# A graph layer with two interleaved parts: the bias of layer h moves from TensorE matmuls to ScalarE, and the split of h into two halves moves to VectorE

## The reference, cut to what matters

```python
h = jnp.maximum(_layernorm(x, axis=-1), 0.0)
S = feat[src]
def edge_nn(x, W, b):
    h = jax.nn.relu(x @ W.T + b)
    return jax.nn.relu(h @ W.T + b)
for r in range(W_rel.shape[0]):
    msgs = jnp.where((rel == r)[:, None], edge_nn(S, W_rel[r], b_rel[r]), msgs)
agg = jax.ops.segment_sum(msgs, dst, num_segments=n_nodes)
gates = agg @ W_ih.T + b_ih + b_hh
i, f, g, o = jnp.split(gates, 4, axis=-1)
c = jax.nn.sigmoid(i) * jnp.tanh(g)
hn = jax.nn.sigmoid(o) * jnp.tanh(c)
x = jax.nn.relu(hn @ W1.T + b1)
x = jax.nn.relu(x @ W2.T + b2)
return x @ W3.T + b3          # added to the input row
```

## Time and profile before

| | |
|---|---|
| median of three runs | 2246.85 us |
| profiled execution, its own time | 2245.49 us |
| its span | 2243.8 us |
| TensorE matmul busy | 2076.3 us, 93% |
| VectorE busy | 1759.5 us, 78% |
| ScalarE busy | 1641.5 us, 73% |
| GpSimd busy | 1182.5 us, 53% |

### The profile page before, as it was taken

One profiled execution on the slowest core, in us unless ns is written; L12 is line 12 of the kernel. 1 busy time (PEld: TensorE's weight loads), 2 busy tenths in 40 slices (PEclk: granted clock), 3 DMA queues, 4 the chain that ended last, 5 costly groups with the idle time before them and its releaser, 6 DMA issues.

```text
span 2243.8 us, 51876 instructions
## 1 busy us (share of the span) xinstructions
PE 2076.3 (93%) x14224; PEld 1397.8 (62%) x14225; DVE 1759.5 (78%) x4311; ACT 1641.5 (73%) x3373; POOL 1182.5 (53%) x917
## 2 busy tenths in 40 slices
PE   5868777768999999999999999999999999999996
PEld 4746555556666666666666666666666666445553
DVE  8657555556888888888888888888888887888886
ACT  3847555557888888888888888888888887666663
POOL 0057777777766666665666666666666644100000
PEclk7669999889999999999999999999999999999998
DMA  9975555558798988898998888898999988998886
GB/s 385 423 244 101 96 99 96 98 95 152 148 181 178 179 166 179 170 180 177 182 182 171 179 173 176 171 176 176 180 179 175 187 153 158 199 189 188 194 192 147
DMA packets 399455, 396.90 MB, mean 177 GB/s; under 512 B 262586, under 2 KB 342006, under 8 KB 393208
## 3 DMA queue, kind: packets, MB, share of 16 engines
q0 software_dynamic: 91200, 157.34, 41.7%
q1 hardware_dynamic: 305636, 238.11, 41.2%
q10 hardware_dynamic: 2516, 0.14, 0.1%
HBM read 185.88 MB, written 156.97 MB: 153 GB/s over the span
## 4 chain that ended last, share of the span: by engine, by line
PE 77%; issue 7%; DMA 6%; POOL 4%; DVE 3%; ACT 3%; POOLq 0%; DVEq 0%; ACTq 0%; SPq 0%
PE bank L1509 33%; PE bank L1456 9%; PE bank L1475 9%; PE bank L1548 6%; PE bank L1523 6%; PE bank L1492 4%; DMA agg<-summed,scatter_idx 4%; PE bank L1438 3%; PE bank L1532 3%; POOL agg L673 2%; POOL xg L657 2%; PE bank L1449 1%; PE bank L1467 1%; DMA a_lo<-row_lo 1%; PE bank L1347 1%
## 5 line engine op out<-in xcount | busy, mean ns | idle before, releaser
L673 POOL DMA_INDIRECT agg<-summed,scatter_idx x400 | 656.4, 1641 | 505.7 <-ACT summed L745 285.2
L1509 PE MATMUL bank<-a_hi,ihT 128*128 128x512 f16 x2400 | 713.8, 379 | 1.7 <-DMA a_lo<-row_lo 1.2
L657 POOL DMA_INDIRECT xg<-in_x,src_ring x384 | 414.2, 1079 | 120.8 <-issue 119.9
L1509 PE MATMUL bank<-a_lo,ihT 128*128 128x512 f16 x1200 | 454.8, 379 | 0.0
L1509 PEld LDWEIGHTS bank<-a_hi,ihT 128*128 128x128 f16 x2400 | 234.4, 98 | 211.9 <-issue 1.4
L1475 PE MATMUL bank<-relT,h_hi 128*128 x1600 | 326.2, 278 | 0.0
L1456 PE MATMUL bank<-s_hi,relT 128*128 128x256 f16 x1600 | 299.8, 282 | 0.0
L681 POOL DMA_DIRECT2D y<-in_x x100 | 133.2, 1332 | 297.7 <-DVE y L1231 287.3
L1456 PE MATMUL bank<-s_lo,relT 128*128 128x256 f16 x800 | 226.2, 283 | 0.0
L1099 DVE SCALAR_TENSOR_TENSOR s_lo<-bank,s_hi 128x512 f16<-128x512 f32 x200 | 136.6, 683 | 111.9 <-ACT s_hi L751 111.9
L1106 DVE SCALAR_TENSOR_TENSOR h_lo<-bank,h_hi 128x512 f16<-128x512 f32 x200 | 137.5, 687 | 110.5 <-ACT h_hi L772 110.5
(11 more groups left out here) (200 smaller groups left out, 4619.6 us busy)
## 6 DMA issues: line engine op xcount, KB each, us to landing
agg_in<-agg SPq DMA_DIRECT2D x100, 512.0 KB, 7.8
y<-in_x POOLq DMA_DIRECT2D x100, 512.0 KB, 9.2
out<-y SPq DMA_DIRECT2D x100, 512.0 KB
agg<-zeros SPq DMA_DIRECT2D x24, 2112.0 KB, 16.0
dst_ring<-dst_rows SPq DMA_DIRECT2D x200, 128.0 KB
agg<-summed,scatter_idx POOLq DMA_INDIRECT x400
xg<-in_x,src_ring POOLq DMA_INDIRECT x384, 5.1
src_ring<-src_slot SPq DMA_DIRECT2D x192, 1.0 KB
```

Of the source, the lines that this page charges most:

```text
L657: nc.gpsimd.indirect_dma_start(out=xg[:, k.slot(8), t, :], out_offset=None, in_=x[:, :], in_offset=bass.IndirectOffsetOnAxis(ap=rows[:, t: ...
L673: nc.gpsimd.indirect_dma_start(out=agg[:, :], out_offset=bass.IndirectOffsetOnAxis(ap=scatter_idx[:, k.slot(8), t:t + 1], axis=0), in_=sum ...
L1509: last = nc.tensor.matmul(N_C[c % 2][:, 0:UNIT], lhs, rhs, start=i == 0, stop=i == len(todo) - 1)
```

## The change

In the joint part the two bias matmuls of layer h go away. ScalarE applies Relu with the bias as a per-partition column, in two instructions of 256 elements (one for each half m) that write a float32 tile `h_f`. VectorE makes `h_hi` from it by a cast and `h_lo` by a subtraction. TensorE's `layer_h` waits for `h_f_ready` of the pair before it, no longer for `h_ready`. The columns stand in a table `pair_bias`, two columns for each pair, which VectorE fills in the preparation from `brel_col`, a 15th weight load. `earlier` now holds 61440 in place of 1, so that the count comes out of ScalarE already multiplied; `marked` with its tile `idx_f` goes away, and `rows_to` makes the row numbers in two instructions of one column each. This holds for edge steps too. VectorE's waits for `gate_ready` in `hidden`, for `idx_f_ready`, for `scattered` in `rows_to` and for `before_ready` in `marked` go (the last moves into `rows_to`).

```diff
-        pair_rel = sb("pair_rel", [1, PAIRS], I32)
+        pair_rel = sb("pair_rel", [P, PAIRS], I32)
+        pair_bias = sb("pair_bias", [P, PAIRS * KH])
...
+            act.dma_start(brel_col[:, :, :], b_rel.rearrange("r (c p) -> p r c", p=P)).then_inc(weights_in, 16)
...
             def high_h(k):
                 if k.within(PAIRS):
                     act.wait_ge(h_done, k.n + 1)
-                    nc.scalar.activation(h_hi[:, k.slot(2), :], B_H[k.bank][:, :], ACT.Relu).then_inc(h_hi_ready, 1)
+                    if k.both:
+                        if k.is_(NB):
+                            act.wait_ge(pair_bias_ready, 1)
+
+                        act.wait_ge(h_ready, k.n)
+                        for m in range(KH):
+                            half = slice(m * PAIR, (m + 1) * PAIR)
+                            last = nc.scalar.activation(h_f[:, half], B_H[k.bank][:, half], ACT.Relu,
+                                                        bias=pair_bias[:, bass.ds(k.n * KH + m, 1)])
+                        last.then_inc(h_f_ready, 1)
+                    else:
+                        nc.scalar.activation(h_hi[:, k.slot(2), :], B_H[k.bank][:, :], ACT.Relu).then_inc(h_hi_ready, 1)
...
-            alternate.then_inc(pair_rel_ready, 1)
+            chained(alternate)
+            nc.vector.tensor_scalar(other_rel[:, :], pair_rel[:, :], 0.0, None, ALU.is_equal).then_inc(pair_rel_ready, 1)
+            dve.wait_ge(pair_rel_ready, 1)
+            dve.wait_ge(weights_in, 16 * WEIGHT_LOADS)
+            for m in range(KH):
+                last = nc.vector.tensor_scalar(other_bias[:, :, m], other_rel[:, :], brel_col[:, 0, m:m + 1], None, ALU.mult)
+            chained(last)
+            bias_of = pair_bias[:, :].rearrange("p (n m) -> p n m", m=KH)
+            for m in range(KH):
+                last = nc.vector.scalar_tensor_tensor(out=bias_of[:, :, m], in0=pair_rel[:, :], scalar=brel_col[:, 1, m:m + 1],
+                                                      in1=other_bias[:, :, m], op0=ALU.mult, op1=ALU.add)
+            last.then_inc(pair_bias_ready, 1)
...
             def low_h(k):
                 if k.within(PAIRS):
+                    if k.both:
+                        dve.wait_ge(h_hi_ready, k.n + 1)
+                        nc.vector.tensor_tensor(h_lo[:, k.slot(2), :], h_f[:, :], h_hi[:, k.slot(2), :],
+                                                ALU.subtract).then_inc(h_ready, 1)
...
+            def high_h(k):
+                if k.within(PAIRS):
+                    dve.wait_ge(h_f_ready, k.n - NB + 1)
+                    nc.vector.tensor_copy(h_hi[:, k.slot(2), :], h_f[:, :]).then_inc(h_hi_ready, 1)
...
-            def marked(k):
+            def rows_to(k):
                 if k.within(PAIRS):
                     dve.wait_ge(before_ready, k.n + 1)
...
+                    for t in range(2):
+                        last = nc.vector.tensor_scalar(scatter_idx[:, k.slot(8), t:t + 1], before[:, k.slot(4), t:t + 1],
+                                                       dst_slot[:, bass.ds(k.n * 2 + t, 1)], spare_row[:, t:t + 1],
+                                                       ALU.add, ALU.min)
+                    last.then_inc(idx_ready, 1)
...
                 if not half:
                     low_rows(k + 1)
+                if (at - 1).both:
+                    high_h(at - 1)
+                hidden(k, half)
                 low_h(at - 1)
-                hidden(k, half)
-                marked(at - 3)
...
-                wait_from(pe, h_ready, k.n if k.both else k.n - 1)
+                if k.is_(NB):
+                    pe.wait_ge(h_ready, k.n)
+                elif k.both:
+                    pe.wait_ge(h_f_ready, k.n - NB)
+                else:
+                    wait_from(pe, h_ready, k.n - 1)
                 for m in range(KH):
                     ps = B_H[k.bank][:, m * PAIR:(m + 1) * PAIR]
-                    nc.tensor.matmul(ps, brel_parts[:, bass.ds(r * D + m * P, P)], ones16[:, :], start=True, stop=False)
+                    if not k.both:
+                        nc.tensor.matmul(ps, brel_parts[:, bass.ds(r * D + m * P, P)], ones16[:, :], start=True, stop=False)
...
-                        last = nc.tensor.matmul(ps, lhs, rhs, start=False, stop=i == len(todo) - 1)
+                        last = nc.tensor.matmul(ps, lhs, rhs, start=k.both and i == 0, stop=i == len(todo) - 1)
```

More of the change, by code:

```diff
@@ L72 @@
 APART = 32768.0
-SPARE = 65536.0
+SPARE = 61440.0
+assert SPARE >= NODES + 2 * P and 0 == SPARE % 32
 FAR = 1.0e6
@@ L93 @@
 CHUNKS = 6
-WEIGHT_LOADS = 14
+WEIGHT_LOADS = 15
 CHUNK_ROWS = [0, 512, 768, 128, 640, 896]
@@ L361, in build @@
         s_lo = sb("s_lo", [P, 2, KH * PAIR], F16)
+        h_f = sb("h_f", [P, KH * PAIR])
         h_hi = sb("h_hi", [P, 2, KH * PAIR], F16)
@@ L370, in build @@
         before = sb("before", [P, 4, 2])
-        idx_f = sb("idx_f", [P, 4, 2])
         scatter_idx = sb("scatter_idx", [P, 8, 2], I32)
@@ L877, in _ @@
                 if t:
-                    nc.vector.memset(earlier[:, same_span(t).start:same_span(t).stop - 1, :], 1.0)
-                nc.vector.tensor_scalar(earlier[:, same_span(t).stop - 1, :], iotaf[:, :], part_id[:, 0:1], None, ALU.is_lt)
+                    nc.vector.memset(earlier[:, same_span(t).start:same_span(t).stop - 1, :], SPARE)
+                nc.vector.tensor_scalar(earlier[:, same_span(t).stop - 1, :], iotaf[:, :], part_id[:, 0:1], SPARE, ALU.is_lt, ALU.mult)
             nc.vector.memset(brel_parts[:, :], 0.0)
@@ L1104, in low_h @@
                 if k.within(PAIRS):
-                    dve.wait_ge(h_hi_ready, k.n + 1)
-                    nc.vector.scalar_tensor_tensor(out=h_lo[:, k.slot(2), :], in0=B_H[k.bank][:, :], scalar=0.0,
-                                                   in1=h_hi[:, k.slot(2), :], op0=ALU.max,
-                                                   op1=ALU.subtract).then_inc(h_ready, 1)
+                    if k.both:
[3 more added lines that the diff above has]
+                    else:
+                        dve.wait_ge(h_hi_ready, k.n + 1)
+                        nc.vector.scalar_tensor_tensor(out=h_lo[:, k.slot(2), :], in0=B_H[k.bank][:, :], scalar=0.0,
+                                                       in1=h_hi[:, k.slot(2), :], op0=ALU.max,
+                                                       op1=ALU.subtract).then_inc(h_ready, 1)
+            def high_h(k):
+                if k.within(PAIRS):
+                    dve.wait_ge(h_f_ready, k.n - NB + 1)
+                    nc.vector.tensor_copy(h_hi[:, k.slot(2), :], h_f[:, :]).then_inc(h_hi_ready, 1)
             def spread_of(k):
@@ L1159, in equal_before @@
                                             ALU.mult).then_inc(same_before_ready, 1)
-            def marked(k):
+            def rows_to(k):
                 if k.within(PAIRS):
                     dve.wait_ge(before_ready, k.n + 1)
-                    nc.vector.scalar_tensor_tensor(out=idx_f[:, k.slot(4), :], in0=before[:, k.slot(4), :], scalar=SPARE,
-                                                   in1=dst_slot[:, bass.ds(k.n * 2, 2)], op0=ALU.mult,
-                                                   op1=ALU.add).then_inc(idx_f_ready, 1)
-            def rows_to(k):
-                if k.within(PAIRS):
-                    dve.wait_ge(idx_f_ready, k.n + 1)
-                    wait_from(dve, scattered, (k.n - 7) * 32)
-                    nc.vector.tensor_tensor(scatter_idx[:, k.slot(8), :], idx_f[:, k.slot(4), :], spare_row[:, :],
-                                            ALU.min).then_inc(idx_ready, 1)
+                    for t in range(2):
[3 more added lines that the diff above has]
+                    last.then_inc(idx_ready, 1)
             def low_rows(k):
```

17 lines of the change are left out of this document (10 added, 7 removed).

## The result

The changed kernel takes 2219.36 us, the median of four runs (2215.95 to 2229.57), against 2247.2 us for the kernel before (four runs, 2246.82 to 2250.77). The ratio is 0.988, with a 95% interval of 0.987 to 0.990: 28 us, or 1.2%, faster. The forecast was 2215.5 us in a range of 2211 to 2224. Two repeats, each beside other runs of the kernel before, gave 2216.9 us (ratio 0.986) and 2216.3 us (0.984); two more runs of the second repeat, 2268.9 and 2287.5 us, were over 1.5% above its fastest and are left out of its median.

A forecast was written before the change was run, and what follows sets the result against it. TensorE, busy for 1331.44 of 1331.59 us, was taken as the bound. The profiled 2245.49 us less 30.8 us of matmuls, other terms 0, gave 2214.7; put nearer the runs' median, the forecast was 2215.5 us, range 2211 to 2224.

The forecast's parts named there:

- Matmul time: TensorE's layer h in the joint part: 278 bias matmuls removed at 0.109 us each, a gain of 30.4 us.
- The 0.4 us for steps 60 and 61: Gain taken for the last four of 14 earlier bias matmuls, in steps that already do gate work.
- ScalarE: Layer h's Relu becomes two of 0.40 us each: 0.32 us a step more, fitting in its idle time.
- The gate behind the table loads: TensorE's third chunk waits for `g_i` after two table loads: 0.12 us of room left, cost 0.
- VectorE: The new cast adds 0.43 us a step, leaving 0.81 of 1.46 us of reserve.
- so they cancel: VectorE's row numbers: dropped `idx_f` against a second `scatter_idx`, 0.15 us each; at worst 0.15 us a step added.
- A unit's low half: Later `h_lo` delays a low half needed by TensorE: with 6.06 us to land, 4.8 us of room.
- The trace shows neither: Claim that neither VectorE's casts nor GpSimd were seen delayed by each other; GpSimd's reserve is 3.7 us a step.
- Rival B: VectorE's cast waits up to 1.6 us for GpSimd: 79 us more, 2325 us; chance 0.05 with anything else slower.
- A: Rival: `h_f` overfills ScalarE's holes, TensorE waits at `g_i` 35 times, 17.5 us, so 2232 us; chance 0.11.
- C: Rival: DMA transfers, busy for 0.88 of the window, are the next bound; time stays at 2246 us; chance 0.05.
- Preparation: VectorE's five added setup instructions, some 2.5 us, and a 15th load are covered by a 20.21 us wait for `mixed`.

The follow-up runs named there:

- d1: Changed kernel with the two bias matmuls of layer h given back, their weights a tile of zeros; 2246.1 us, ratio 0.999 to the kernel before.
- e3: Changed kernel with three more Relus of 256 elements, results unused, behind the two of `h_f` in every joint step; 2222.4 us, ratio 0.989.
- a1: Changed kernel with `marked`, `idx_f` and the old `rows_to` put back, so the bias part alone; 2222.6 us, ratio 0.990.
- b1: Kernel before the change with only the new row numbers; 2247.7 us, ratio 1.000.
- j1: Changed kernel with VectorE's `low_s`, which reads a bank, moved between `row_lo` and the cast `h_hi`; 2216.8 us, ratio 0.985.
- k1: Changed kernel unaltered, run once more beside others on the same chip; 2216.3 us, ratio 0.984.
- f1: Changed kernel with `h_hi` made by a maximum of `h_f` with itself in place of the cast; 2223.1 us, ratio 0.989.
- c1: Changed kernel unaltered, run again in more rounds; 2216.9 us, ratio 0.986.
- i1: Changed kernel with VectorE's `rows_to` (row numbers) moved between `h_lo` and the cast `hn_hi`; 2218.6 us, ratio 0.987.
- g1: Changed kernel with the cast of h done twice, the second result unused; 2229.5 us, ratio 0.991.

## Why the prediction was right, and where not

**Matmul time.** 30.4 us for 278 matmuls was right: 29.48 us for the 270 of 135 steps, and d1 gives it all back. The 0.4 us for steps 60 and 61 can't be seen beside a variation of 5 us ahead of step 64.

**ScalarE.** The two Relus start 0.36 us apart, not 0.40 (1190.89, and `g_o` at 1191.61, 0.72 for both). So the step got 0.24 us more, not 0.32. The hole before `g_o` was forecast at about 0.1 and is 0.22, that before `x` stayed (0.45 against 0.44).

**The gate behind the table loads.** `g_i` ends at 1208.19, 0.28 us more is 1208.47, and the low load came at 1208.59: 0.12 us of room, as forecast, and no wait. e3 showed that this is the place that decides, and that I had counted each hole 0.1 us too small.

**VectorE.** The total was right by luck: from step 64 to 199 VectorE is busy for 8.69 us a step in place of 8.23, 0.47 more, and 0.43 was forecast. Two errors made it up. The cast lasts 423 ns in the median, as taken, but the bias part alone (a1) adds only 0.25 us a step: behind the cast the next instruction starts after 0.34 us, and `h_lo` now has one close behind it. The step that failed is "so they cancel" for the row numbers. From start to start they went from some 0.15 us for the old pair to 0.36 for the two new ones (264 ns each in the median), and b1 has 0.22 us a step more; I had bounded this term at 0.15. (The 84 us more between 600 and 1840 us aren't the price of the change: that window holds three steps more than before.) Behind the hole before `rstd`, which is gone as forecast (a total of 1.8 us in the span against 37.0), nothing more was left to take it, but nothing urgent stands there either. VectorE's reserve is 0.75 us a step, 0.81 was forecast.

**A unit's low half.** The room of 4.8 us came from one landing of 6.06 us, and that one stands behind the last pair, where only units are left. In the joint part landings of 12.54 and 18.24 us exist, and TensorE waited for both. Between steps 64 and 199 the term was 0 in the profiles of after, a1, j1 and k1, 1.3 us in f1, 1.6 in c1, 10 in i1, and in g1 a wait of 2.8 us with the low clock behind it. It belongs in the sum as a tail, not as nothing.

**GpSimd.** "The trace shows neither" was wrong for GpSimd's side. I looked at VectorE's casts only, and 82 of GpSimd's gathers and scatters from 600 to 1840 us were already longer by part of a VectorE instruction. Rival B's sentence that the delay can fall on GpSimd is what happened, but not through the cast alone: `h_lo`, now read from SBUF, closes the row. The longest gather went from 1.86 to 4.83 us. The Trainium skill (SBUF — State Buffer, section "SBUF: two separate sides") names VectorE instructions with two inputs in SBUF as well, but only against a GpSimd instruction that reads SBUF. In this case they delay indirect gathers and scatters, 82 already in the kernel before. No cast of `h_hi` took over 0.707 us, so the delay falls on the engine with 3.7 us of reserve, and costs nothing.

**Rivals A and C** did not happen. A's mechanism is real, as e3 shows, but 1.07 us a step beyond the 0.24 of the change cost only 4.9 us. C falls with the unchanged DMA share at a shorter step.

**Preparation.** The five instructions took 1.6 us (102.69 to 104.27, 2.5 taken), and the wait for `mixed` went from 20.21 to 18.40 us, so they are hidden.

## What to carry to other kernels

Where one engine is busy without a gap over a long window, work taken from it counts in full, and the test for it is to give that work back with zeros for data. For the engines that take the work over, look for the shortest chain between two of the bound engine's waits, not at their mean idle time, and count a hole as its printed length plus the overlap that it suppresses. When a VectorE operand moves from PSUM to SBUF, look at GpSimd's DMAs: a long unbroken row of two-input instructions and casts between SBUF tiles can delay them by up to the whole row, and a small or PSUM-reading instruction put into the middle cuts it.

## What the hardware showed that was not expected

- The gathers that VectorE delays end 0.90 us after the end of one of its instructions between SBUF tiles (two inputs, or a cast), the scatters 1.48 us after it. Some stand over a whole row of such instructions, others only over the first: 26 and 22 of the 48 gathers that started during `row_lo` in the changed kernel. The longest went from 1.86 to 4.83 us (gather), and from 2.38 to 5.41 us (scatter, between 600 and 1840 us).
- Two VectorE instructions on one column with two column operands took 0.36 us from start to start, more than twice the 0.15 us that the pair of two columns had taken together.
- The transposes of a unit's low half took 12.54 us to land in step 72 of c1 and 18.24 in step 72 of i1; TensorE waited 1.4 and 7.11 us. In most profiles it never waited for one in these steps.
- Behind 7.11 us of idle time TensorE's granted clock was 0.50 for some 5 us, and its matmuls took twice as long; behind 1.40 us it stayed at 1.00.
